# Feeding the layer-norm statistics of the last stage from a bf16 copy instead of from f32

## The reference

```python
x = _layernorm(x + _L0_attn_ref(x, ...), axis=-1)
x = _layernorm(x + _L0_ffn_ref(x, L0_ffn_weights, L0_ffn_scale, L0_ffn_bias), axis=-1)

def _L0_ffn_ref(x, weights, scale, bias):
    w = (weights >= 0.0).astype(x.dtype) * 2.0 - 1.0
    y = jnp.einsum('bsi,oi->bso', x, w)
    y = y * scale + bias
    return jnp.clip(y, -MAX_VAL, MAX_VAL)

def _layernorm(x, axis=-1, eps=1e-5):
    m = jnp.mean(x, axis=axis, keepdims=True)
    v = jnp.var(x, axis=axis, keepdims=True)
    return (x - m) / jnp.sqrt(v + eps)
```

## Time and profile before

| what | value |
|---|---|
| time before, median of 2 runs | 807.43 us (768.67 and 846.19) |
| the profiled execution, its own time | 771.73 us |
| its span, slowest core (core 4) | 770.2 us |
| spans of the 8 cores | 746.9 to 770.2 us |
| busy share of the span | PE 83%, DVE 42%, ACT 46%, POOL 6% |
| mean granted TensorE clock of core 4 | 0.944 of full speed |
| chain of work that ended last | PE 65%, DMA 17%, DVE 8%, ACT 5%, issue 4% |

### The profile page before, as it was taken

How to read it: one execution, slowest core, us unless ns; L and a number is a source line. 1 busy time by engine, 2 the same in 40 slices (tenths; PEclk the granted TensorE clock), 3 DMA queues, 4 the chain that set the end, 5 groups by cost and what they waited for, 6 DMA issues and landing times.

```text
span 770.2 us, 7276 instructions; the slowest of 8 cores (746.9 to 770.2 us)
## 1 busy us (share of the span) xinstructions
PE 641.8 (83%) x2752; PEld 266.4 (35%) x2752; DVE 319.8 (42%) x178; ACT 354.2 (46%) x262; POOL 48.7 (6%) x92
## 2 busy tenths in 40 slices
PE   0459999999999999999998679979978799767610
PEld 0014444444444444444443334433323242222100
DVE  0000000007676876767732202133486592564163
ACT  2442233337868778677713202124643675534510
POOL 2010000000000000001212111000000000000000
PEclk9999999999999999999999979999998899898955
DMA  8995000012222222225199988157420000121024
GB/s 184 242 196 90 1 1 0 1 14 41 43 40 31 40 42 42 35 34 83 14 169 199 210 148 169 49 171 217 156 86 1 1 0 1 54 96 69 0 70 149
DMA packets 23218, 61.34 MB, mean 80 GB/s; under 512 B 2704, under 2 KB 2704, under 8 KB 23184
## 3 DMA queue, kind: packets, MB, share of 16 engines
q0 software_dynamic: 12672, 23.07, 21.1%
q1 hardware_dynamic: 8208, 29.42, 12.4%
q10 hardware_dynamic: 2304, 8.39, 3.7%
HBM read 75.55 MB, written 8.39 MB: 109 GB/s over the span
## 4 chain that ended last, share of the span: by engine, by line
PE 65%; DMA 17%; DVE 8%; ACT 5%; issue 4%; SPq 0%; ACTq 0%; DVEq 0%; POOLq 0%
PE psA L152 33%; PE psB L152 32%; DMA A<-x 6%; DMA A<-Wof 4%; DMA A<-Wob 3%; DVE A L721 2%; DMA out<-A 2%; DMA A<-Wffn 2%; DVE A L785 2%; DVE A L714 1%; ACT A L780 1%; ACT A L867 1%; DVE srows L613 1%; ACT srows L616 1%; DVE A L685 1%
## 5 line engine op out<-in xcount | busy, mean ns | idle before, releaser
L152 PE MATMUL psA<-A 128*128 128x512 bf16 x1536 | 362.1, 394 | 70.6 <-ACT A L331 22.1
L152 PEld LDWEIGHTS psA<-A 128*128 128x128 bf16 x1536 | 150.9, 100 | 276.3 <-issue 112.1
L152 PE MATMUL psB<-A 128*128 128x512 bf16 x1024 | 227.6, 381 | 1.9 <-DVE A L570 1.9
L152 PEld LDWEIGHTS psB<-A 128*128 128x128 bf16 x1024 | 100.5, 98 | 124.3 <-issue 4.6
L431 DVE TENSOR_SCALAR A<-A,dvec_sb 128x2048 f32<-128x2048 f32 x16 | 20.6, 1286 | 169.2 <-ACT A L427 169.2
L152 PE MATMUL psB<-A,ones_sb 128*1 128x512 bf16 (+1 forms) x160 | 51.6, 467 | 7.6 <-ACT A L888 5.6
L442 DVE TENSOR_TENSOR A<-A 128x2048 f32<-128x2048 f32 x16 | 36.7, 2292 | 51.0 <-ACT A L435 51.0
L575 ACT ACTIVATE A<-A,dvec_sb 128x1024 bf16<-128x1024 f32 x16 | 18.4, 1148 | 81.5 <-DVE A L570 81.5
L427 ACT ACTIVATE A<-psB,vecs_sb 128x2048 f32<-128x2048 f32 x16 | 31.5, 1967 | 31.9 <-PE psB L152 31.9
L433 ACT ACTIVATE A<-A 128x2048 f32<-128x2048 f32 x16 | 30.6, 1910 | 23.8 <-DVE A L431 23.8
L570 DVE SCALAR_TENSOR_TENSOR A<-psA,A 128x1024 f32<-128x1024 f32 x8 | 9.8, 1225 | 72.1 <-PE psA L152 59.6
(11 more groups left out here) (54 smaller groups left out, 337.9 us busy)
## 6 DMA issues: line engine op xcount, KB each, us to landing
A<-x SPq DMA_DIRECT2D x40, 512.0 KB, 8.5
A<-x ACTq DMA_DIRECT2D x8, 512.0 KB, 14.6
A<-Wof POOLq DMA_DIRECT2D x16, 256.0 KB, 11.1
A<-Wob POOLq DMA_DIRECT2D x16, 256.0 KB, 13.5
A<-Wffn SPq DMA_DIRECT2D x8, 512.0 KB, 5.4
out<-A ACTq DMA_DIRECT2D x8, 512.0 KB, 4.1
out<-A SPq DMA_DIRECT2D x8, 512.0 KB, 4.0
A<-Wxf POOLq DMA_DIRECT2D x8, 256.0 KB, 31.8
```

The lines of the kernel that those rows point to most:

```text
L152: inst = e.matmul(oa, lh, rh, start=st, stop=sp)
```

## The change

The two sums over r2 in `_stats` no longer read the f32 r2. Each block gets one more ACT operation directly behind the DVE operation that writes r2: a Copy (L886 in the changed kernel) of r2 from f32 to a bf16 buffer `r2bf`, one buffer for each of the 8 blocks, laid over a region of A5 that is free by then. The Square and the sum matmuls read this bf16 copy, and the f32 column of ones and its memset at the kernel's start are dropped. DVE's output r2 stays f32, and the final layer norm still reads it. Line numbers shift by -2 to +7: L867, L873, L879, L888 and L728 are L868, L874, L879, L895 and L726 in the changed kernel.

```diff
-    def stats_tiles(src_ap_fn, src_buf, k, slot, f32=False):
-        lh = ones32_sb.ap() if f32 else ones_sb.ap()
+    def stats_tiles(src_ap_fn, src_buf, k, slot):
         tiles, treads = [], []
         for t in range(2):
-            tiles.append((lh, src_ap_fn(k, t),
+            tiles.append((ones_sb.ap()[:],
+                          src_ap_fn(k, t),
...
         r2B = rA3.new(f"r2h{h}", CH)
+        r2bfB = [new_over(rR1e[k:k + 1], f"r2bfh{h}_{k}") for k in range(CH)]
+        r2bf_ap8 = [A5.ap()[:, R1 // 2 + k * 1024: R1 // 2 + (k + 1) * 1024]
+                    for k in range(CH)]
...
                   reads=[uB[sl], x1B[o]], writes=[r2B[o]] + war, inc="dv")
+            bd.op("scalar",
+                  lambda e, o=o: e.activation(r2bf_ap8[o],
+                                              r2f[:, o * 1024:(o + 1) * 1024],
+                                              AF.Copy),
+                  reads=[r2B[o]], writes=[r2bfB[o]], inc="sc")
+
             def _stats(o=o):
                 sl = o % 2
                 bd.op("scalar",
                       lambda e, o=o, sl=sl:
-                      e.activation(rsq_ap[sl], r2f[:, o * 1024:(o + 1) * 1024],
-                                   AF.Square),
-                      reads=[r2B[o]], writes=[rsqB[sl]], inc="sc")
-                stats_tiles(lambda k, t:
-                            r2f[:, k * 1024 + t * 512: k * 1024 + (t + 1) * 512],
-                            r2B[o], o, 2, f32=True)
+                      e.activation(rsq_ap[sl], r2bf_ap8[o], AF.Square),
+                      reads=[r2bfB[o]], writes=[rsqB[sl]], inc="sc")
+                stats_tiles(lambda k, t: r2bf_ap8[k][:, t * 512:(t + 1) * 512],
+                            r2bfB[o], o, 2)
                 stats_tiles(lambda k, t, sl=sl: rsq_ap[sl][:, t * 512:(t + 1) * 512],
                             rsqB[sl], o, 3)
```

More of the change, by code:

```diff
@@ L193, in build_program @@
     onesb_sb = nc.alloc_sbuf_tensor("onesb_sb", [1, 128], BF16)
-    ones32_sb = nc.alloc_sbuf_tensor("ones32_sb", [128, 1], F32)
     srbf = nc.alloc_sbuf_tensor("srbf", [1, 4096], BF16)
@@ L324, in build_program @@
     bd.op("vector", lambda e: e.memset(onesb_sb[:], 1.0), writes=[onesB], inc="dv")
-    bd.op("vector", lambda e: e.memset(ones32_sb[:], 1.0), writes=[onesB], inc="dv")
     for i in range(2 * CH):
```

## The result

The changed kernel takes 786.51 us (median of 11 runs) against 768.84 us before (10 runs): ratio 1.0214, 95% interval 1.0182 to 1.0247. It is slower, by more than the runs' own scatter; whether by more than 2% is not settled, since 1.02 lies inside the interval. The ratio is of the 8 and 9 of these runs that are not in the chip's second state, in which four cores or all eight show a lower granted clock and the time is some per cent longer. The forecast of 786.9 us met the time itself, but 0.52 of its chances lay on "within 2%", which the prediction took for a change that can't be told from none, and this one can. The profiled execution took 784.87 us, span 783.3 us on its slowest core, core 1.

The account below looks back on a forecast made before the run. It took PE to bound half 0 and a ring over ACT, DVE and the DMA issue half 1's loop. From 771.73 us, +9.5 (half 0), +7.5 (half 1 loop) and -1.8 (its flush) gave 786.9 us, range 779 to 793.

Parts of the forecast that it names:

- What bounds the kernel: Last stage: PE bounds half 0 at 3.70 us a block; half 1's loop is not PE-bound, only its flush is.
- the ring over DVE and the DMA issue: Half 1's loop: ACT's four Relus, DVE, the output DMA's issue on ACT's queue, ACT again; 11.24 us a turn.
- The Copy's own cost: On ACT in the last stage: 1.05 us a Copy, 0.96 us back to back, 15.4 us for 16.
- The wait that the Copy brings: In both loops each block becomes a serial chain: 4.86 us odd, 5.74 us even in half 0; half 1 +2.51 us a turn.
- The flushes and the clock: Ends of both halves: 4.6 us of PE idle lowers its clock, costing 2.4 us each; half 1's flush -1.8 us.
- The rival in which the clock holds: Both flushes: the gap ahead does not lower PE's clock; +11.6 us, 783.3 us; chance 0.22.
- The rival in which the clock is low through half 0's loop: PE's clock also low between half 0's blocks: +4.5 us, 791.4 us; chance of the clock low for longer 0.18.
- The other side: Copies hide under PE's 3.70 us a block in half 0: L611 4.8 us earlier, half 1 some 5; 762 us; chance 0.08.
- The sum: Whole kernel: 771.73 + 9.5 + 7.5 - 1.8 = 786.9 us, with the line for slower at 787.2.
- this likeliest case: The forecast as summed, 786.9 us for the whole kernel; chance 0.40.
- The parts named for "slower": Slower by over 2%, above 787.2 us: half of the forecast, the low clock and something slower than all; chance 0.43.

Follow-up runs that it names:

- r2 in bf16: The changed kernel without the Copy: DVE writes r2 itself as bf16, read by sums, squares and the final layer norm; 756.17 us, ratio to before 0.9838.
- The Copy alone: The kernel before with the 16 Copies added behind DVE's r2 and read by nobody, squares and sums still on f32 r2; ratio to before 1.0316.
- the filler: The changed kernel with 16 more matmuls, read by nobody, on PE ahead of each flush; ratio to before 1.0144, stage 125.5 us.

## Why the prediction was wrong in its verdict and right in its sum

**What bounds the kernel.** Right: PE in half 0, the ring over DVE and the DMA issue in half 1. It rests on the waits (1.01 us for PE in the earlier trace rows, 6.47 us for DVE in the earlier trace rows) and on what the experiments lengthened. That half 1's loop stays at 33.7 us with r2 in bf16 proves nothing for it, since no sum stands in that stretch. One reading was off: PE's pace in half 0 is 3.45 us a block, the distance of the Relus, and not 3.70. The row of 22.21 us for 96 matmuls begins at a mean clock of 0.74 (609.79 to 615 us). So the Copies would have hidden only below a wait of 3.45 - 3.31 = 0.14 us, not 0.4.

**The Copy's own cost.** Right, 1.06 us each (forecast 1.05), and right that it is not what counts: with the same Copies the stage is 15.6 us longer than before at one place, 0.8 us longer at another and 3.0 us shorter at the third.

**The wait that the Copy brings.** Right: 4.81 us an odd block (forecast 4.86), 5.73 us an even one (5.74), a turn of 13.73 us (11.24 + 2.51 = 13.75). The Copy alone gives the same loops with the old sums.

**The flushes and the clock.** The idle ahead of each flush was 4.72 us (I had 4.6), the clock fell to 0.50, and the loss that I charged as a whole, 2.4 us, was 2.1 and 3.1 by the filler. The rival in which the clock holds falls; the filler is what it would look like. The rival in which the clock is low through half 0's loop came about in its clock and not in its price: the two blocks behind the 2.12 us gap took 8.75 us where two take 7.07 in the kernel with r2 in bf16, and the clock was 0.50 from 631.5 to 633.5 us (core 1). So what I had concluded from the one gap of 2.54 us, that gaps this short leave the clock alone, was wrong. But the Relus did not come later for it, since a block's matmuls run ahead of the Relu that they serve. I had priced that rival as if PE were the bound there, which it was not.

**The other side** (Copies hidden) would have needed another place in ACT's queue. With the Copy one block late it comes true by 3 us, and with the Copy off ACT by 9.7, about what the rival had in all (4.8 and 5).

**The step that failed** is the one from the sum to the chances, in "The sum": "2% of it is 15.4 us, about what a measurement of this kernel can tell from no change; the line for slower is 787.2". It took 2% for the limit of a measurement, without a row for it. The interval of the ratio turned out 0.3% either way, so a rise of 15 us in 770 is told from none with ease, and the runs show one of 14 to 19 us. The sum had said +15.2 us, and still half of this likeliest case, and the whole of the one in which the clock holds (+11.6 us), went to "within 2%". The line itself was also misplaced: it came from the one profiled execution, 771.73 us, where the runs have a median of 768.84 us, so that 2% above it is 784.2 us and the forecast of 786.9 us lies beyond. On which side of 2% the changed kernel lies the interval (1.0182 to 1.0247) leaves open. (The parts named for "slower" add to 0.42, not 0.43.)

**What was luck.** The sum was 0.4 us short in the stage. That 786.9 met 786.51 as closely is partly luck: the time that I started from was 2.9 us above the median of the runs, and the slowest core's rise of 17.7 us (below) was 2.5 us above my sum.

**What stays open.** The slowest core's time rose by 17.7 us between the medians (766.9 us of span over 18 executions, 784.6 over 9), the mean over the cores by 16.4 (756.1 to 772.5), and the stage by 15.6. The first core to reach the stage and the last differ by some 20 us in every trace, and which core ends last changes from one execution to the next. The interval of the ratio (1.0182 to 1.0247, +14.0 to +19.0 us) holds all three figures, and no run was made to tell the 2 us apart. Open too is what decides the clock behind a gap of some 2 us (see the last section).

## What to carry to other kernels

An instruction in an in-order queue costs the time that its input is late, paid by all that stands behind it. Before moving work to an engine with a low busy share, write out the new chain of one block (here ACT, DVE, ACT) and compare it with the bound of that stage; then look for the place in the queue where the input has been ready for long: one block later was worth 21 us here. A gain on an engine counts only where something waits for that engine: of 19.5 us saved on PE, 12 at most came through. Take the line that separates "same" from "slower" from several executions, and compare stretches of the trace rather than spans when a few microseconds decide.

## What the hardware showed that I had not expected

**GpSimd and DVE shut each other out.** A 128x1024 cast on GpSimd takes 1.04 us with DVE idle, as fast as on ACT. Issued at 620.54 while DVE ran L683 (two inputs, until 622.62), it ended at 623.51, 0.9 us after DVE; and DVE's next operation L690, from 622.72, took 2.94 us instead of 2.29, about the time until the cast's end and then its own. Each waited for about the whole of the other (the times on POOL are rough, those on DVE are not). This is what the Trainium skill, SBUF — State Buffer, section "SBUF: two separate sides", says: the port pair that the two share is an exclusive lock, for a DVE operation with two SBUF inputs among others, not a split of bandwidth. In this kernel it costs DVE 0.65 to 0.83 us an operation, and does not undo the gain.

**A matmul group that does nothing useful paid for itself** where it closed a gap of 4.7 us to 1.1 us: 5.2 us less in the stage. Gaps of 1.08 us left the clock at 1.00, and 4.72 us of idle was followed by 0.50, with 22 matmuls in 7.6 to 8.0 us in both flushes of all 8 cores.

**The length of the gap does not settle the clock.** Gaps of 2.25 us went either way. With r2 in bf16 the 22 matmuls behind such a gap took 5.43 us on cores 1 and 3 and 6.8 to 6.9 us on the other six, in both halves. With the Copy on GpSimd they took 5.43 us on all 8 cores in half 1, while in half 0, behind 2.26 us, five of the 8 cores needed 6.8 to 6.9 us. What decides it, no run here shows.

**The output stage differs by die in one execution**: 39.6 us on cores 0 to 3 and 45 us on cores 4 to 7 with the same program, the difference lying in the waits for output DMAs. What sets it, no run here shows.
